# Cross-attention and LoRA-MoE on one core: three of eight delta additions of the last two pairs by way of ScalarE and GpSimd, and the sum of squares ahead of delta on TensorE

## The chip, the cores and the metric

The kernel runs on one core of one Trainium2 chip. The metric is the device time of the program in microseconds (us). The median of 3 runs of the kernel before is 455.8 us (454.64 to 456.86).

## What is computed

x and ctx are (8, 512, 2048) float32. Cut to what matters:

```python
x = x + xattn(layernorm(x), ctx, ctx)     # 8 heads of 64 channels: softmax over the head's channels for q,
                                          # over the 2048 positions for k; kv = k^T v, out = q kv
h = layernorm(x)
gates  = softmax of the top 2 of h @ router_w.T         # 4 experts
mid    = einsum('tf,erf->ter', h, A)                    # rank 16
x = x + 4 * einsum('te,ter,eor->to', gates, mid, B)     # "delta"
```

## The kernel before, in words

The 4096 rows (b, c) make 32 tiles of 128 (NT = 32), two tiles make a pair (NP = 16). A tile's 2048 columns are worked on in 16 chunks of 128, four chunks being a quarter. Every engine runs the same loop over steps q from -8 to 153, and each helper decides from q which tile and quarter (or pair) is its own, so the order on every engine is fixed by hand. Engines wait for each other by counting semaphores; each engine executes its own program in order.

For a tile: GpSimd subtracts the key maximum from ctx (`shift`, L311), ScalarE takes exponentials of keys and queries, TensorE makes kv and the numerator, VectorE normalises into `attnT` (L700), and GpSimd adds attnT to x, which gives x1 in `y_sb` (`add_x`, L323; four `attnT` slots, one for each quarter). ScalarE squares x1 (L544), TensorE folds the squares (`fold_squares`, L438), ScalarE copies the folded rows to `sq_sum` (`copy_squares`, L564), and TensorE sums them into a column of `raw_ps` (`sum_squares`, L448). `project` (L423) puts mid and the router's logits into the same `raw_ps`.

For a pair, p, the gates follow on single steps. At q = 8p+17: `gate_centre` (VectorE, L716 and L717, waits for the sum of squares of both tiles) makes the negative mean and E[x^2]; `root2` (GpSimd, L338 to L343) makes 1/sqrt(var); VectorE's `gate_logits` and `gate_below`. At 8p+18: VectorE's `gate_beats`, `gate_mask`, `gate_rank` (L758), ScalarE's `gate_exp` (L574, waits for root2), VectorE's `gate_select` (L763, waits for rank and exp), `gate_sum`, `gate_scale`. At 8p+19: `gate_mid` (L786), TensorE's `turn_mid` (L457). At 8p+20: `mid_high` (ScalarE, L583) and `mid_low` (VectorE, L800). From q = 8p+21 on `delta`: the pair's delta in eight groups i = 0 to 7, one a step. A group is four matmuls (L471 and L472) into one of two banks, `delta_ps[i % 2]`. VectorE adds it to `y_sb` (`add_delta`, L709) and frees the bank by counting `out_made`; TensorE's group i waits until group i-2 is added. Group i of pair p is written D(p,i) below. D(14,i) has q = 133+i and D(15,i) has q = 141+i. So the gates of pair 15 (q = 137 to 140) lie among the groups of pair 14.

Within a step TensorE issues delta, turn_max, sum_squares, numerator, spread_kmax, kv, project, fold_squares, turn_mid. The sums of squares of tiles 29, 30 and 31 have q = 128, 132 and 136. VectorE issues gate_beats(0), gate_mid, the maxima, kv_recip, gate_centre, gate_beats(1), gate_mask, mid_low, bn_part, add_delta, gate_logits, gate_rank, normalise, gate_below, gate_select, gate_sum, gate_scale. GpSimd issues root1, shift, root2, add_x.

SyncE issues all DMAs in order. For pair 14 two stores of 512 KB wait for the first four groups, and two (L243) for all eight; then pair 15 goes out in eight stores of 256 KB, one for each group (`store_last`, L248).

Of the kernel before, what the change touches and what calls it, by code (L numbers as in the profile page):

```python
# [6 lines left out]
ALU = mybir.AluOpType  # L7
# [32 lines left out]
def after(eng, sem, value):  # L40
    if value > 0:
        eng.wait_ge(sem, value)


def xattn_lora_moe_kernel(nc, x, xt, ctxt, wt, bt, consts, out):
# [7 lines left out]
    x_rows = x.rearrange("b c n -> (b c) n")  # L53
    FIRST = -8
    LAST = 4 * (NT - 1) + 29

    with ExitStack() as stack:
        def sb(name, shape, dt=F32):
# [5 lines left out]
        def sem(name):  # L64
            return stack.enter_context(nc.semaphore(name))
# [100 lines left out]
        rden_made = sem("rden_made")  # L166
        attn_made = sem("attn_made")
        out_made = sem("out_made")
        b_lo_made = sem("b_lo_made")
        negmean2_made = sem("negmean2_made")  # L170
        ex2_made = sem("ex2_made")
# [24 lines left out]
        def tile_at(q, offset):  # L196

            t, g = divmod(q - offset, 4)
            return (t, g) if 0 <= t < NT else (None, g)
# [6 lines left out]
        def delta_at(q):  # L206
            p, i = divmod(q - 21, 8)
            return (p, i) if 0 <= p < NP else (None, i)

        def chunks(g):  # L210
            return slice(g * CH, (g + 1) * CH)
# [4 lines left out]
        def pair_slots(p):  # L216
            return slice(2 * (p % 4), 2 * (p % 4) + 2)
# [3 lines left out]
        @block.sync  # L221
        def _(sp):
            PIECES = 2
            CP = NCH // 2 // PIECES
            XW = N // PIECES
            YC = NCH // PIECES

            def load_ctx(t, k):
                c = slice(k * CP, (k + 1) * CP)
                sp.dma_start(ctx_sb[:, t % 4, c, :, :].rearrange("p a c b -> p a (c b)"),  # L230
                             ctxt[t][:, c, :, :].rearrange("p a c b -> p a (c b)")).then_inc(ctx_landed[t % 4], 16)

            def load_x(t, k):
                c = slice(k * XW, (k + 1) * XW)
                sp.dma_start(x_sb[:, t % 4, c], x_rows[t * P:(t + 1) * P, c]).then_inc(x_landed[t % 4], 16)  # L235

            def load_y(t, k):
                c = slice(k * YC, (k + 1) * YC)
                sp.dma_start(y_sb[:, t % 8, c, :], xt[t][:, c, :]).then_inc(y_landed[t % 8], 16)

            def store(t, k):
                c = slice(k * YC, (k + 1) * YC)
                sp.dma_start(out[t, :, c, :].rearrange("p j c -> p (j c)"),  # L243
                             y_sb[:, t % 8, c, :].rearrange("p j c -> p (j c)")).then_inc(out_stored[t % 8], 16)

            def store_last(i):
                c = slice(2 * i, 2 * i + 2)
                sp.dma_start(out[NT - 2:NT, :, c, :].rearrange("t p j c -> p t (j c)"),  # L248
                             y_sb[:, pair_slots(NP - 1), c, :].rearrange("p t j c -> p t (j c)")
                             ).then_inc(last_stored, 16)  # L250

            def whole(load, t):
                for k in range(PIECES):
                    load(t, k)

            def quarters_done(q, offset):

                return min(q - offset + 1, 4 * NT)

            sp.dma_start(cst[:], consts).then_inc(cst_landed, 16)  # L260
            whole(load_ctx, 0)
            whole(load_x, 0)
            whole(load_ctx, 1)
            sp.dma_start(w_sb[:], wt).then_inc(w_landed, 16)
            whole(load_x, 1)
            whole(load_ctx, 2)
            whole(load_y, 0)
            sp.dma_start(b_rows, bt).then_inc(b_landed, 16)
            whole(load_y, 1)
            whole(load_x, 2)  # L270
            whole(load_ctx, 3)
            STEP = 4 // PIECES
            for q in range(0, 4 * NT + 28, STEP):
                last = q + STEP - 1
                p, r = divmod(q - 26, 8)
                if 0 <= p < NP - 1:
                    t, k = 2 * p + r // STEP % 2, r // (2 * STEP)
                    after(sp, raw_done, quarters_done(q - 1, 7))
                    sp.wait_ge(out_made, 8 * p + 8 // PIECES * (k + 1))
                    store(t, k)  # L280
                t, r = divmod(q + 10, 4)
                if 3 <= t < NT:
                    after(sp, num_done, 4 * (t - 4) + r + STEP)
                    load_x(t, r // STEP)
                t, r = divmod(q, 4)
                if 2 <= t < NT:
                    after(sp, raw_done, quarters_done(q, 7))
                    if t >= 8:
                        sp.wait_ge(out_stored[t % 8], 16 * PIECES * (t // 8))
                    load_y(t, r // STEP)  # L290
                t, r = divmod(q + 16, 4)
                if t < NT:
                    sp.wait_ge(kv_done, 4 * (t - 4) + r + STEP)
                    load_ctx(t, r // STEP)
            for i in range(8):
                sp.wait_ge(out_made, 8 * (NP - 1) + i + 1)
                store_last(i)
            for k in range(8):
                uses = len(range(k, NT - 2, 8))
                sp.wait_ge(out_stored[k], 16 * PIECES * uses)  # L300
            sp.wait_ge(last_stored, 16 * 8)

        @block.gpsimd
        def _(pool):
# [28 lines left out]
            def root2(q):  # L333
                p = pair_at(q, 13)
                if p is None:
# [7 lines left out]
                pool.tensor_tensor(rstd2[:], var2e[:], minus_half.to_broadcast([P, 2]),  # L343
                                   ALU.pow).then_inc(rstd2_made, 1)

            pool.memset(kv_sb[:], 0.0).then_inc(kv_zeroed, 1)
            pool.wait_ge(kv_zeroed, 1)
            for h in range(2):
# [4 lines left out]
            for q in range(FIRST, LAST + 1):  # L353
                root1(q)
                shift(*tile_at(q, -3))
                root2(q)
                add_x(*tile_at(q, 5))

        @block.tensor
        def _(pe):  # L360
# [98 lines left out]
            def delta(p, i):  # L459
                if p is None:  # L460
                    return
                if i == 0:
                    pe.wait_ge(lo_made, p + 1)
                    if p == 0:
                        pe.wait_ge(b_hi_made, 1)
                        pe.wait_ge(b_lo_made, 4)
                after(pe, out_made, 8 * p + i - 1)
                for k in range(2):
                    j = 2 * i + k
                    to = delta_ps[i % 2][:, k * 2 * P:(k + 1) * 2 * P]  # L470
                    pe.matmul(to, b_hi[:, j * P:(j + 1) * P], midT[:, p % 2, :], start=True, stop=False)  # L471
                    mm = pe.matmul(to, b_lo[:, j * P:(j + 1) * P], midT[:, p % 2, :], start=False, stop=True)  # L472
                mm.then_inc(delta_done, 1)
# [8 lines left out]
            for _ in range(40):  # L482
                pe.transpose(raw_ps[0][:, 0, 0:P], ident, ident)
            for q in range(FIRST, LAST + 1):
                delta(*delta_at(q))
                turn_max(q)
                sum_squares(q)
                if q == 1:
                    sum_w()
                numerator(*tile_at(q, 5))  # L490
                spread_kmax(q)
                kv(*tile_at(q, 0))
                project(*tile_at(q, 7))
                fold_squares(q)
                turn_mid(q)

        @block.scalar
        def _(act):
# [68 lines left out]
            def gate_exp(q):  # L567
# [5 lines left out]
                for d in range(2):  # L573
                    act.activation(gexp[:, d, :], below_max[:, d, :], ACT.Exp,  # L574
                                   scale=rstd2[:, d:d + 1]).then_inc(gexp_made, 1)

            def mid_high(q):
                p = pair_at(q, 16)
                if p is None:
                    return  # L580
                act.wait_ge(midT_done, 2 * p + 2)
                after(act, delta_done, 8 * (p - 1))
                act.activation(midT[:, p % 2, :].rearrange("p (d c) -> p d c", d=2),  # L583
                               raw_ps[p % 2][:, :, COL_MID:COL_MID + P], ACT.Copy).then_inc(hi_made, 1)
# [4 lines left out]
            for q in range(FIRST, LAST + 1):  # L589
# [14 lines left out]
                if r == 3:  # L604
                    copy_squares(T - 2)
                    keys(T + 1, 0)
                    queries(T, 0)
                if q == 2:
                    act.wait_ge(w_summed, 1)
                    act.activation(w_mean[:], raw_ps[1][:, 0, 0:ER + E], ACT.Copy,  # L610
                                   scale=1.0 / N).then_inc(w_mean_made, 1)
# [5 lines left out]
        def _(dve):  # L617
# [85 lines left out]

            def add_delta(p, i):
                if p is None:
                    return
                dve.wait_ge(delta_done, 8 * p + i + 1)
                y = y_sb[:, pair_slots(p), 2 * i:2 * i + 2, :]
                dve.tensor_tensor(y, delta_ps[i % 2][:].rearrange("p (j t c) -> p t j c", j=2, t=2), y,  # L709
                                  ALU.add).then_inc(out_made, 1)  # L710
# [186 lines left out]
```

## Time and profile before

| | us |
|---|---|
| median of 3 runs | 455.8 (454.64 to 456.86) |
| profiled execution | 454.94 |
| its span, first to last instruction | 453.2 |
| TensorE matmul busy | 422.5 (93%) |
| VectorE busy | 379.1 (84%) |
| GpSimd busy | 358.9 (79%) |
| ScalarE busy | 311.0 (69%) |

The profile is one execution; the median is over other executions of the same program. Busy times don't count waiting. In the rows PE is TensorE's matmuls, PEld its weight loads, DVE VectorE, ACT ScalarE, POOL GpSimd, SP SyncE, and SPq the queue of DMAs that SyncE issues. The granted clock is a share of TensorE's full 2.4 GHz.

### The profile page before, as it was taken

The numbers are of one execution on the slowest core, as the hardware profiler recorded it, in microseconds if no ns is written. First come the engines' busy times: TensorE is split into PE (matmuls) and PEld (weight loads), VectorE is DVE, ScalarE is ACT, GpSimd is POOL, SyncE is SP. The second block draws the span as 40 slices with busy tenths as digits, with TensorE's granted clock in tenths as the row PEclk, the third lists the DMA queues.
The fourth block names the chain that finished last, engine by engine and source line by source line (L and its number), as shares of the span: only waits on it lengthen the run. The fifth ranks groups of instructions, "written<-read, shape, count | busy, mean of one in ns | idle before, by whom it ended". The sixth has DMA issues, their size and how long they took to land.

```text
span 453.2 us, 16801 instructions
## 1 busy us (share of the span) xinstructions
PE 422.5 (93%) x6888; PEld 382.3 (84%) x6888; DVE 379.1 (84%) x1045; ACT 311.0 (69%) x436; POOL 358.9 (79%) x343
## 2 busy tenths in 40 slices
PE   6558998999999999999999999999999999999975
PEld 6557887898989898998989898998989898999864
DVE  3468777898998989898998989898989989775864
ACT  1265979695968778695958777785959777775310
POOL 0466999999898989898898989898988988994610
PEclk9667999999999999999999999999999999999988
DMA  8995888779999999999999999999999998454247
GB/s 286 420 409 188 307 290 271 248 276 321 364 297 372 339 340 344 307 341 332 351 310 361 331 346 341 307 352 333 357 316 338 310 366 269 173 186 187 95 185 279
DMA packets 38972, 137.59 MB, mean 304 GB/s; under 512 B 4208, under 2 KB 6384, under 8 KB 38768
## 3 DMA queue, kind: packets, MB, share of 16 engines
q1 hardware_dynamic: 38896, 136.52, 86.5%
q8 instruction: 55, 0.90, 0.8%
q14 instruction: 21, 0.17, 0.1%
HBM read 102.95 MB, written 33.55 MB: 301 GB/s over the span
## 4 chain that ended last, share of the span: by engine, by line
PE 71%; DVE 10%; POOL 6%; DMA 4%; issue 3%; SPq 3%; ACT 1%; POOLq 0%; DVEq 0%; ACTq 0%
PE num_ps L407 21%; PE kv_ps L390 14%; PE raw_ps L423 11%; PE delta_ps L471 10%; PE kv_ps L438 6%; PE delta_ps L472 6%; DMA ctx_sb<-in_ctxt_dram 4%; DVE y_sb L709 3%; POOL y_sb L323 3%; POOL ek_sb L311 3%; DVE attnT L700 2%; DVE bn_parts L642 2%; DVE midT L800 1%; PE raw_ps L457 1%; SPq L235 1%
## 5 line engine op out<-in xcount | busy, mean ns | idle before, releaser
L311 POOL TENSOR_TENSOR ek_sb<-ctx_sb,kmax_row 128x512 f32<-128x512 f32 x128 | 167.8, 1313 | 36.5 <-ACT kmax_row L504 36.5
L323 POOL TENSOR_TENSOR y_sb<-attnT,y_sb 128x512 f32<-128x512 f32 x128 | 164.3, 1284 | 31.0 <-DVE attnT L700 31.0
L407 PE MATMUL num_ps<-kv_sb,x_sb 128*128 128x130 f32 x1024 | 141.1, 281 | 9.0 <-DVE attnT L700 6.0
L407 PEld LDWEIGHTS num_ps<-kv_sb,x_sb 128*128 128x128 f32 x1024 | 126.0, 192 | 12.9 <-issue 8.7
L709 DVE TENSOR_TENSOR y_sb<-delta_ps,y_sb 128x512 f32<-128x512 f32 x128 | 87.3, 684 | 23.7 <-PE delta_ps L472 22.8
L625 DVE TENSOR_REDUCE max_n<-ctx_sb 128x32 f32<-128x512 f32 x128 | 86.5, 677 | 10.8 <-DMA ctx_sb<-in_ctxt_dram 10.8
L390 PE MATMUL kv_ps<-ctx_sb,ek_sb 128*64 128x65 f32 x2048 | 92.8, 233 | 0.3 <-ACT ek_sb L526 0.3
L700 DVE TENSOR_TENSOR attnT<-num_ps,rden 128x512 f32<-128x512 f32 x128 | 88.5, 691 | 4.8 <-DVE rden L697 0.4
L390 PEld LDWEIGHTS kv_ps<-ctx_sb,ek_sb 128*64 128x64 f32 x2048 | 74.2, 139 | 17.8 <-issue 5.8
L526 ACT ACTIVATE ek_sb<-ek_sb 128x1024 f32<-128x1024 f32 x64 | 67.1, 1049 | 26.9 <-POOL ek_sb L311 26.9
L423 PE MATMUL raw_ps<-w_sb,y_sb 128*64 128x69 f32 x2048 | 84.5, 223 | 0.0
L471 PE MATMUL delta_ps<-midT,b_hi 128*128 128x256 f32 x256 | 81.1, 338 | 0.6 <-DVE y_sb L709 0.4
L533 ACT ACTIVATE x_sb<-x_sb,nbias,rstd 128x1024 f32<-128x1024 f32 x64 | 78.8, 1231 | 0.0
L423 PEld LDWEIGHTS raw_ps<-w_sb,y_sb 128*64 128x64 f32 x2048 | 73.1, 136 | 0.9
L472 PE MATMUL delta_ps<-midT,b_lo 128*128 128x256 f32 x256 | 68.0, 287 | 0.0
L471 PEld LDWEIGHTS delta_ps<-midT,b_hi 128*128 128x128 f32 x256 | 49.5, 193 | 13.2 <-issue 5.8
L472 PEld LDWEIGHTS delta_ps<-midT,b_lo 128*128 128x128 f32 x256 | 50.0, 195 | 0.0
L642 DVE BATCH_NORM_STATS2 bn_parts<-x_sb 128x6 f32<-128x512 f32 x64 | 43.9, 686 | 1.0 <-DMA x_sb<-in_x_dram 0.5
L544 ACT ACTIVATE sq_b<-y_sb 128x1024 f32<-128x1024 f32 x32 | 33.7, 1052 | 6.1 <-POOL y_sb L323 6.1
L564 ACT ACTIVATE sq_sum<-kv_ps 128x128 f32<-128x128 f32 x32 | 8.5, 266 | 38.3 <-PE kv_ps L438 38.3
L697 DVE RECIPROCAL rden<-num_ps 128x8 f32<-128x8 f32 x128 | 25.7, 201 | 10.6 <-PE num_ps L407 9.8
L544 ACT ACTIVATE sq_a<-y_sb 128x1024 f32<-128x1024 f32 x32 | 33.5, 1048 | 0.0
(63 smaller groups left out, 398.3 us busy)
## 6 DMA issues: line engine op xcount, KB each, us to landing
ctx_sb<-in_ctxt_dram SPq DMA_DIRECT2D x64, 520.0 KB, 5.3
x_sb<-in_x_dram SPq DMA_DIRECT2D x64, 512.0 KB, 6.1
y_sb<-in_xt_dram SPq DMA_DIRECT2D x64, 512.0 KB, 6.3
out_dram<-y_sb SPq DMA_DIRECT2D x60, 512.0 KB, 6.2
out_dram<-y_sb SPq DMA_DIRECT2D x8, 256.0 KB, 3.6
sq_a<-in_bt_dram SPq DMA_DIRECT2D x1, 1024.0 KB, 15.8
w_sb<-in_wt_dram SPq DMA_DIRECT2D x1, 552.0 KB, 9.6
cst<-in_consts_dram SPq DMA_DIRECT2D x1, 145.0 KB, 2.3
```

Source lines behind the costliest of these rows:

```text
L311: pool.tensor_tensor(ek_sb[:, t % 2, chunks(g), :].rearrange("p (a b) c -> p a b c", b=2), ctx_sb[:, t % 4, 2 * g:2 * g + 2, 1:P + 1, :].r ...
L323: pool.tensor_tensor(y, attnT[:, g, :], y, ALU.add).then_inc(x1_made, 1)
L390: mm = pe.matmul(kv_ps[t % 2][d, h:h + DH + 1], ek_sb[:, t % 2, j, d], ctx_sb[:, t % 4, j // 2, v, j % 2], start=(j == 0), stop=(j == NCH ...
L407: mm = pe.matmul(num_ps[:, j // 2, at:at + 2 * (DH + 1)], x_sb[:, t % 4, c * P:(c + 1) * P], kv_sb[:, t % 2, :], start=True, stop=True, sk ...
L423: mm = pe.matmul(raw_ps[p % 2][c, odd, 0:NQ], y_sb[:, t % 8, j, c], w_sb[:, j, :], start=(odd == 0 and j == 0), stop=(j == NCH - 1), skip_ ...
L471: pe.matmul(to, b_hi[:, j * P:(j + 1) * P], midT[:, p % 2, :], start=True, stop=False)
L472: mm = pe.matmul(to, b_lo[:, j * P:(j + 1) * P], midT[:, p % 2, :], start=False, stop=True)
L533: act.activation(half, half, ACT.Exp, bias=nbias1[:, t % 4:t % 4 + 1], scale=rstd1[:, t % 4:t % 4 + 1]).then_inc(q_made, 1)
L544: act.activation(to, y_sb[:, t % 8, 8 * h:8 * h + 8, :].rearrange("p j c -> p (j c)"), ACT.Square).then_inc(sq_made, 1)
L625: dve.tensor_reduce(max_n[:, t % 2, c], ctx_sb[:, t % 4, :, 1 + g * 32:33 + g * 32, :].rearrange("p a c b -> p c a b"), AX.XY, ALU.max).th ...
L700: dve.tensor_tensor(attnT[:, g, :].rearrange("p (b k d) -> p b k d", b=2, d=DH), heads[:, :, :, 0:DH], rden[:].unsqueeze(3).to_broadcast([ ...
L709: dve.tensor_tensor(y, delta_ps[i % 2][:].rearrange("p (j t c) -> p t j c", j=2, t=2), y, ALU.add).then_inc(out_made, 1)
```

## The change

In pairs NP-2 = 14 and NP-1 = 15, three groups each (1, 3, 5 and 0, 2, 4) are no longer added by VectorE. ScalarE copies the bank into one of the four `attnT` slots (`copy_delta`, after all of x1 has been made), which frees the bank (`delta_copied`), and GpSimd adds the slot to `y_sb` (`add_delta_late`, last in its step). `adds_until` says how many adds up to a group are VectorE's and how many the other way's; SyncE's stores and TensorE's delta wait for both counts. From q = 4 NT = 128 on, TensorE issues sum_squares ahead of delta.

```diff
@@ kernel
+    BY_POOL = {NP - 2: (1, 3, 5), NP - 1: (0, 2, 4)}
...
+        def by_pool(p, i):
+            return i in BY_POOL.get(p, ())
+
+        def adds_until(p, i):
+
+            n = 8 * p + i + 1
+            shared = sum(1 for pair in BY_POOL for k in BY_POOL[pair] if 8 * pair + k < n)
+            return n - shared, shared
@@ SyncE, store of pairs 0 to 14
-                    sp.wait_ge(out_made, 8 * p + 8 // PIECES * (k + 1))
+                    by_dve, shared = adds_until(p, 8 // PIECES * (k + 1) - 1)
+                    sp.wait_ge(out_made, by_dve)
+                    after(sp, out_made_pool, shared)
@@ SyncE, the last eight stores
-                sp.wait_ge(out_made, 8 * (NP - 1) + i + 1)
+                by_dve, shared = adds_until(NP - 1, i)
+                sp.wait_ge(out_made, by_dve)
+                after(sp, out_made_pool, shared)
                 store_last(i)
@@ GpSimd
+            def add_delta_late(p, i):
+
+                if p is None or not by_pool(p, i):
+                    return
+                n = adds_until(p, i)[1]
+                pool.wait_ge(delta_copied, n)
+                y = y_sb[:, pair_slots(p), 2 * i:2 * i + 2, :]
+                pool.tensor_tensor(y, attnT[:, (n - 1) % 4, :].rearrange("p (j t c) -> p t j c", j=2, t=2), y,
+                                   ALU.add).then_inc(out_made_pool, 1)
...
                 root2(q)
                 add_x(*tile_at(q, 5))
+                add_delta_late(*delta_at(q))
@@ TensorE, delta
-                after(pe, out_made, 8 * p + i - 1)
+                by_dve, shared = adds_until(p, i - 2)
+                after(pe, out_made, by_dve)
+                after(pe, delta_copied, shared)
@@ TensorE, the loop
             for q in range(FIRST, LAST + 1):
+                if q >= 4 * NT:
+                    sum_squares(q)
                 delta(*delta_at(q))
                 turn_max(q)
-                sum_squares(q)
+                if q < 4 * NT:
+                    sum_squares(q)
@@ ScalarE
+            def copy_delta(p, i):
+
+                if p is None or not by_pool(p, i):
+                    return
+                n = adds_until(p, i)[1]
+                act.wait_ge(x1_made, 4 * NT)
+                after(act, out_made_pool, n - 4)
+                act.wait_ge(delta_done, 8 * p + i + 1)
+                act.activation(attnT[:, (n - 1) % 4, :], delta_ps[i % 2][:], ACT.Copy).then_inc(delta_copied, 1)
...
                     keys(T + 1, 0)
                     queries(T, 0)
+                copy_delta(*delta_at(q))
@@ VectorE, add_delta
                 if p is None:
                     return
+                if by_pool(p, i):
+                    return
```

## Rows read from the trace of the kernel before

**Rows 1.** Busy time by stretch (us, instructions; then granted clock, DMA share, GB/s).
```profile
300.00:400.00 100.00, 98.31 (x1678) 89.38 (x1670) 90.10 (x254) 75.53 (x107) 88.22 (x85) 1.00 0.90 309
...
434.00:440.00 6.00, 3.28 (x22) 2.73 (x21) 5.44 (x21) 0.49 (x3) 1.10 (x3) 0.88 0.45 178
440.00:446.00 6.00, 5.92 (x26) 5.07 (x26) 3.98 (x7) 0.38 (x1) 0.00 (x0) 0.55 0.60 226
```

**Rows 2.** Chain of waits, 437 to 442: start, us, what ran.
```profile
437.47 0.23 DVE raw_ps L758
...
437.72 0.18 DVE gsel L763
...
438.73 0.50 DVE mid L786 x2
...
439.27 0.70 PE raw_ps L457 x2
...
440.41 0.44 DVE midT L800
...
440.90 0.58 PE delta_ps L471
441.48 0.21 PE delta_ps L472
```

**Rows 3.** Busy time by stretch, 442 to 452.
```profile
442.00:443.00 1.00, 1.00 (x6) 0.78 (x5) 0.69 (x1) 0.00 (x0) 0.00 (x0) 0.50 0.56 225
443.00:444.00 1.00, 1.00 (x5) 1.00 (x6) 0.69 (x1) 0.00 (x0) 0.00 (x0) 0.50 1.00 401
...
450.00:451.00 1.00, 0.00 (x0) 0.00 (x0) 0.00 (x0) 0.00 (x0) 0.00 (x0) 1.00 1.02 350
451.00:452.00 1.00, 0.00 (x0) 0.00 (x0) 0.00 (x0) 0.00 (x0) 0.00 (x0) 1.00 0.37 128
```

**Rows 4.** Instructions in order of time, 433 to 437: start, us, engine, line.
```profile
433.28 0.28 ACT L564 ACTIVATE sq_sum<-kv_ps 128x128 f32<-128x128 f32 x1 [1.20 <-PE kv_ps L438]
...
433.93 1.29 DVE L709 TENSOR_TENSOR y_sb<-delta_ps,y_sb 128x512 f32<-128x512 f32 x2 [1.92 <-PE delta_ps L472]
...
434.09 0.28 PE L472 MATMUL delta_ps<-midT,b_lo 128*128 128x256 f32 x1
...
434.20 0.28 PE L448 MATMUL raw_ps<-cst,sq_sum 128*128 128x2 f32 x2
...
435.13 0.15 DVE L716 TENSOR_SCALAR negmean<-raw_ps 128x2 f32<-128x2 f32 x1
...
435.36 0.19 POOL L338 TENSOR_TENSOR mean_sq<-negmean 128x2 f32<-128x2 f32 x1 [4.37 <-DVE negmean L716]
...
435.97 0.71 POOL L343 TENSOR_TENSOR rstd<-var2e,cst 128x2 f32<-128x2 f32 x1
...
436.71 0.49 ACT L574 ACTIVATE gexp<-below_max,rstd 128x4 f32<-128x4 f32 x2 [3.15 <-POOL rstd L343]
```

**Rows 5.** Groups by line and shape, 395 to 453: count | busy, mean ns.
```profile
L323 POOL TENSOR_TENSOR y_sb<-attnT,y_sb 128x512 f32<-128x512 f32 x13 | 16.6, 1278 | 10.6 <-DVE attnT L700 10.6
...
L533 ACT ACTIVATE x_sb<-x_sb,nbias,rstd 128x1024 f32<-128x1024 f32 x5 | 6.1, 1229 | 0.0
...
L544 ACT ACTIVATE sq_b<-y_sb 128x1024 f32<-128x1024 f32 x4 | 4.2, 1055 | 6.1 <-POOL y_sb L323 6.1
...
L583 ACT ACTIVATE midT<-raw_ps 128x256 fp32r<-128x256 f32 x3 | 1.2, 385 | 5.3 <-PE raw_ps L457 5.3
```

**Rows 6.** Last stores and adds: order of time, then the store line's own view.
```profile
441.64 0.81 SPq L243 DMA_DIRECT2D out_dram<-y_sb  x2
...
447.42 1.33 DVE L709 TENSOR_TENSOR y_sb<-delta_ps,y_sb 128x512 f32<-128x512 f32 x2 [0.19 <-PE delta_ps L472]
...
L248 SPq DMA_DIRECT2D out_dram<-y_sb x8: 401/496/1062, 442.9 to 448.8; - x8
...
DMA to landing us min/median/max: 3.1/3.6/4.0
```

More of the change, by code:

```diff
@@ L168, in xattn_lora_moe_kernel @@
         out_made = sem("out_made")
+        out_made_pool = sem("out_made_pool")
+        delta_copied = sem("delta_copied")
         b_lo_made = sem("b_lo_made")
```

## The prediction

> D(p,i) is delta group i of pair p, and the step numbers q are those of the section on the kernel. Times are us from the start of the span.
>
> **What bounds the kernel now.** I read the busy time by stretch first. In the body (300 to 400) TensorE is busy 98.3 of 100 us at full clock; none of the diff's branches fires there, since GpSimd takes groups of pairs 14 and 15 alone and the order on TensorE changes only from q = 128 on. At the end the picture is another: TensorE is busy 3.28 of 6.00 between 434 and 440, where VectorE is busy 5.44, and 5.92 of 6.00 between 440 and 446, at a granted clock of 0.55 (nearly all of it at 1.2 GHz of 2.4) [rows 1]. So only the last 20 us are at stake, and in their middle a serial chain counts. The chain of waits shows it: softmax gates of pair 15 on VectorE (gsel at 437.72, mid at 438.73), the transpose of mid on TensorE at 439.27, the high part on ScalarE, the low part on VectorE at 440.41, and D(15,0) on TensorE at 440.90 [rows 2]. Third, the DMA by stretch: share 0.56 in 442:443, 1.00 in 443:444, 1.02 in 450:451, 0.37 in 451:452 [rows 3]. The last 3.1 MB (two stores of 512 KB, eight of 256 KB) leave in one unbroken stream. It starts when D(14,7) is added, as the two large stores wait for it and D(14,7) stands behind the transpose of mid on TensorE. Hence the end follows the moment at which the gate chain of pair 15 is through, nearly whatever the adds of pair 15 do.
>
> **Parts that move nothing.** The extra waits of SyncE and TensorE split one semaphore's count over two; for pairs 0 to 13 the second has the value zero and isn't waited for. Sum_squares at q = 128 and 132 goes ahead of D(13,3) and D(13,7): the same two short matmuls, 0.28 in the record [rows 4], in either place. VectorE reads the first a step later, behind a normalise that waits for TensorE anyway, and the second only with tile 31's. Zero for both; were that cover gone, under 0.28 each.
>
> **The squares of tile 31 (q = 136).** Before, D(14,3) runs first (its last matmul 434.09 to 434.37) and the sum of squares starts at 434.20 and is done at 434.48 [rows 4]. Its input sq_sum is made at 433.28 + 0.28 = 433.56, before D(14,3)'s first matmul, three steps of 0.12 (as from 434.09 to 434.20) ahead of its last: 433.73. So in the new order it starts at 433.73 and is done at 434.01, and D(14,3) is done two such steps later, at 434.60. By itself this earlier sum is worth nothing: gate_centre starts at 435.13, well behind it, because VectorE is in two adds from 433.93 on for 1.29 [rows 4]. With D(14,3)'s add gone from VectorE, gate_centre can start after one of them, at about 434.55, 0.58 earlier.
>
> **The price of a copy and of a GpSimd add.** An ACT copy of 128x512 from PSUM isn't in the trace. Nearest below: 128x128 from PSUM, 0.28 [rows 4]; above: 128x1024 in SBUF, 1.055, and with bias and scale 1.229 [rows 5]. On the line between the copy of 128x256 from PSUM (0.385) and the 1024 wide one, 512 is 0.385 + 256 x (1.055 - 0.385)/768 = 0.61. I take 0.60; the ends are 0.28 and 1.23. The GpSimd add has the size and both SBUF inputs of L323: 1.28 [rows 5], and its ends are that and the 1.30 to which I round it up for the other pattern of columns. VectorE did two in 1.29.
> The Trainium skill, page "ScalarE: Activation LUTs", section "Rules for kernel authors", budgets about 0.3 us for an ACTIVATE plus 0.83 ns an element, an estimate of 0.73 for the copy; for the 1024 wide ones it gives 1.15, where the trace has 1.055 and 1.229. By that rule the shift below would be 0.77 where the rows give 0.64.
>
> **The stall that the change adds.** The copy of D(14,1) on ScalarE falls into the 1.20 for which that engine is idle ahead of copy_squares at 433.28 [rows 4]; it runs 432.1 to 432.7, so that isn't late. GpSimd's add is 432.75 to 434.03. The second is the one that bites: D(14,3) is done at 434.60, copied by 435.22, added on GpSimd 435.25 to 436.53. In GpSimd's program this add (q = 136) stands ahead of root2 of pair 15 (q = 137). Root2 began at 435.36 with mean_sq, its power ended at 435.97 + 0.71 = 436.68, and exp began at 436.71 [rows 4]. Now root2 starts at 436.50, 1.14 later, although its input is ready 0.58 earlier. So the power ends at 437.82, exp runs 437.85 to 438.34, and gate_select, at 437.72 before, waits for it and starts at 438.36: **0.64 late**. VectorE can't win that back: the three adds taken off it lie ahead of this wait (rank, at 437.47 before [rows 2], would start at about 437.0). Behind gate_select all steps shift by the 0.64: mid at 439.37, transpose at 439.91, D(15,0) at 441.54 [rows 2]. D(14,5)'s copy stands behind exp on ScalarE and is done at about 438.95, its GpSimd add at 440.25: TensorE needs the bank for D(14,7) only after the transpose, and SyncE wants the add at 442.2. Both covered by over a microsecond. The stores of the first half of pair 14 go out once D(14,3) is added, at 436.6, five microseconds ahead of the next ones, into a half idle stretch of the DMA engines: nothing.
>
> **The drain of pair 15.** D(14,7) is added by 442.2 where it was by 441.6, so the two large stores leave from 442.28 on (were from 441.64 on [rows 6]), and the stream begins at 443.1 instead of 442.45 (a share of 0.56 in 442:443 [rows 3]). TensorE at the low clock spends 4 x 0.215 = 0.86 on a group [rows 2]. With two engines emptying the two banks, each bank is free about when TensorE comes back: group starts at 441.54, 442.40, 443.26, 444.23, 445.09, 446.04, then, at the full clock, 446.74 and 447.46. VectorE's last add ends at 448.82; before it was 447.42 + 1.33 = 448.75 [rows 6]. VectorE's share of the drain thus wins the 0.64 back but for 0.07. But the store of an even group waits for copy and GpSimd: D(15,4) is copied by 446.7 and added by 448.0, so its store is issued at 448.05; SyncE issues in order, and the four last stores, 0.50 each [rows 6], come at 448.05, 448.55, 449.05 and 449.55. The last was at 448.8. The stream needs its 8.9 us (442.45 to 451.37 before [rows 3]) from 443.1 on and ends at 452.0, and no store comes so late that the engines run dry by more than 0.1. A store's landing, 3.1 to 4.0 [rows 6], holds that queueing already. Either reading gives 0.6 to 0.75 later.
>
> **Sum.** Body 0; squares 0; root2 behind the second GpSimd add +0.64; drain 0 on the stream of stores: span 453.2 + 0.64 = 453.8. The profiled execution took 454.94 (1.74 around the span), so 455.6 for it. It lies 0.86 under the median of the timed runs, so for the median I forecast 455.8 + 0.64 = 456.4. With a copy at 0.28 the shift is 0.32, with 1.23 it is 1.27 and the drain no longer hides.
>
> **Rivals.**
> *The intended gain arrives.* If root2 isn't held, gate_select comes with rank, whose start falls from 437.47 [rows 2] to about 437.0 since D(14,5)'s add is gone: 0.5 earlier, span 452.7, median 455.3. For it: VectorE is the busy engine between 434 and 440 [rows 1]. Against: to have exp done by 437.2 GpSimd must start its add by 434.1, and D(14,3) isn't in PSUM then. Chance 0.12.
> *The stream of stores decides alone, nothing moves.* If stores that come spread out leave at the 401 GB/s of 443:444 rather than at the 350 of 450:451 [rows 3], a stream of 3.1 MB is shorter by up to 1.1 and makes up for the later start; half of that leaves the end within 0.1 of before: 455.8. For it: those two rates. Against: all the bytes must still leave after a later start. Chance 0.15.
> *The copy holds the banks; slower beyond what can be told.* Place: the copy of even groups of pair 15, in front of TensorE's next even group. At 1.23 a copy, TensorE waits 0.6 more before D(15,2), D(15,4) and D(15,6), of which 1.2 stays, and root2 comes another 0.63 late: 0.64 + 0.63 + 1.2 = 2.5, span 455.7, median 458.3. It decides from a copy of about 0.85, where TensorE's 0.86 no longer covers it. Against: the line through the two PSUM copies, 0.28 and 0.385 for 128 and 256 columns, gives 0.60 for 512. Chance 0.07.
> *The clock stays low.* Granted clock is 0.55 in 440:446 [rows 1] after the idle ahead of the transpose; that idle grows by 0.64. If the full clock doesn't come back before the end, the last three groups take 0.86 each: last add 449.4 to 449.9, span 454.4 to 454.9, median about 457.2. For it: the gap grows. Against: TensorE then works as densely as before. Chance 0.11.
> The Trainium skill, page "TensorE: Matmul & The Clock Gate", section "What's actually happening", says that the gated clock is the default and that activity lifts it, which fits the fall after the idle in this trace and would favour this last case.
>
> **Chances and range.** Forecast 0.55, the four rivals 0.12, 0.15, 0.07 and 0.11. All but one lie within 0.5% (2.3 us), about what a measurement of this kernel can tell from no change; the timed runs of one kernel lay 2.2 apart. Faster by over 0.5%: 0.04, for the spread of a median alone. Slower by over 0.5%: 0.07. Within: 0.89. Range 454.6 to 458.0: from the gain with 0.7 of spread below it to the low clock with 0.8 above.
>
> **What would show it.** Right: on GpSimd, the add of D(14,3) followed without a gap by mean_sq at about 436.5; ScalarE's exp and VectorE's gsel at 437.85 and 438.4, with gsel released by exp; D(15,0) at about 441.5; copies of 0.6; stores ending at 449.5 or later. Wrong: mean_sq before 435.4, gsel under 437.7, D(15,0) before 440.9 or after 442.2, copies above 0.85, or a difference ahead of 425.

## The result and the profile after

The changed kernel is slower: median 458.10 us of 22 runs against 456.59 us for the kernel before, ratio 1.0045 (95% interval 1.0029 to 1.0062), that is 2.0 us (1.3 to 2.8). A second series gave 1.0032 (1.0017 to 1.0047), 1.5 us. Together, each series weighted by its interval, about 1.7 us. The forecast was +0.64 on a median of 455.8 from three runs; 22 runs put that median at 456.59. The three-run median was 0.8 low.

The profiled execution of the changed kernel took 457.65 us. The page's head:

```profile
span 455.9 us, 16833 instructions
...
PE 422.8 (93%) x6888; PEld 382.4 (84%) x6888; DVE 375.1 (82%) x1039; ACT 314.6 (69%) x442; POOL 366.9 (80%) x349
```

The span is 2.7 longer, but that isn't the change. Up to the last normalise of tile 31 (VectorE, attnT) both kernels execute the same instructions in the same order, except for where two sums of squares (q = 128 and 132, two short matmuls each) stand. It came at 428.94 before and here at:

```profile
430.32 0.69 DVE L743 TENSOR_TENSOR attnT<-num_ps,rden 128x512 f32<-128x512 f32 x1
```

1.38 later. The prediction named a difference ahead of 425 as a sign of being wrong, so this needs a reason. Over the 17 profiles of this document it lies between 428.94 and 432.25: 428.94 to 430.91 in the five kernels that leave the squares in their old place, 429.00 to 432.25 in the twelve others, so it doesn't follow the change. It goes with the time that TensorE spent at the low clock ahead of it: 20.5 us in five profiles, with the last normalise at 428.9 to 430.2, and 30.7 us in six, with it at 430.3 to 432.3 (correlation 0.8 over the 17). Part of it is visible in the granted clock at the start, here after and then before, stretch 20:40 (us; busy by engine; granted clock, DMA share, GB/s):

```profile
20.00:40.00 20.00, 15.25 (x125) 13.77 (x124) 12.96 (x24) 10.50 (x13) 9.20 (x7) 0.50 0.85 334
```

```profile
20.00:40.00 20.00, 14.40 (x130) 12.99 (x131) 13.06 (x25) 10.50 (x13) 9.21 (x7) 0.60 0.84 331
```

So every time below is counted **from the start of the last normalise** ("from N"). The tail from N to the end is 24.2 before and 25.6 after, 1.3 more (24.21 and 25.55). In order of time (start, us, engine, line), the part that answers to [rows 4]:

```profile
434.66 0.28 ACT L596 ACTIVATE sq_sum<-kv_ps 128x128 f32<-128x128 f32 x1 [0.71 <-PE kv_ps L465]
...
435.10 0.28 PE L475 MATMUL raw_ps<-cst,sq_sum 128*128 128x2 f32 x2
...
435.30 0.69 DVE L754 TENSOR_TENSOR y_sb<-delta_ps,y_sb 128x512 f32<-128x512 f32 x1 [3.22 <-PE delta_ps L501]
...
435.91 0.15 DVE L761 TENSOR_SCALAR negmean<-raw_ps 128x2 f32<-128x2 f32 x1
...
436.06 0.60 ACT L617 ACTIVATE attnT<-delta_ps 128x512 f32<-128x512 f32 x1 [1.12 <-PE delta_ps L501]
...
436.74 1.28 POOL L369 TENSOR_TENSOR y_sb<-attnT,y_sb 128x512 f32<-128x512 f32 x1 [1.43 <-ACT attnT L617]
...
437.97 0.20 POOL L354 TENSOR_TENSOR mean_sq<-negmean 128x2 f32<-128x2 f32 x1
...
438.36 0.23 DVE L803 TENSOR_REDUCE raw_ps<-beats_m 128x8 f32<-128x64 f32 x1
438.59 0.71 POOL L359 TENSOR_TENSOR rstd<-var2e,cst 128x2 f32<-128x2 f32 x1
439.33 0.48 ACT L606 ACTIVATE gexp<-below_max,rstd 128x4 f32<-128x4 f32 x2 [2.67 <-POOL rstd L359]
...
439.92 0.17 DVE L808 SCALAR_TENSOR_TENSOR gsel<-raw_ps,gexp 128x8 f32<-128x8 f32 x1 [1.33 <-ACT gexp L606]
...
441.46 0.44 PE L484 MATMUL raw_ps<-cst,mid 128*128 128x128 f32 x2 [3.16 <-DVE mid L831]
...
442.84 0.58 PE L500 MATMUL delta_ps<-midT,b_hi 128*128 128x256 f32 x1 [0.46 <-DVE midT L845]
```

The sum of squares (L475) is ahead of D(14,3), and gate_centre starts 5.59 from N (6.19 before). Its result waits: GpSimd is in the add of D(14,3) and starts mean_sq with the add's end, at 7.65 (6.42 before). Rank is ready at 8.04, but gate_select starts at 9.60 and follows exp, where before it was 8.78 and followed rank: 0.82 late. D(15,0) starts at 12.52 (11.96), only 0.56 late. The other 0.26 came back between them, since the transpose of mid (L484) took 0.44 at the full clock where it took 0.70 at the low one before [rows 2].

The last stores: SyncE's queue in order of time, the store line's own view (ns min/median/max of an issue) and the DMA in two stretches, against [rows 6] and [rows 3]:

```profile
446.18 6.31 SPq L260 DMA_DIRECT2D out_dram<-y_sb  x8
```

```profile
L260 SPq DMA_DIRECT2D out_dram<-y_sb x8: 372/422/1157, 446.2 to 452.0; - x8
...
DMA to landing us min/median/max: 2.3/3.1/3.5
```

```profile
448.00:449.00 1.00, 0.61 (x6) 0.51 (x5) 0.69 (x1) 0.38 (x1) 0.71 (x2) 1.00 0.70 231
...
451.00:452.00 1.00, 0.00 (x0) 0.00 (x0) 0.00 (x0) 0.00 (x0) 0.00 (x0) 1.00 0.57 190
```

VectorE's last add ends at 20.24 from N (19.81 before), the last store is issued at 452.0, 21.7 from N (19.9 before). The DMA engines ran dry twice, share 0.70 and 0.57, where the stream had been unbroken. Over the whole stream, from the first packet of the two large stores to the last packet of all, before and then after:

```profile
442.46:452.33 9.87, 5.41 (x27) 4.35 (x26) 5.12 (x8) 0.00 (x0) 0.00 (x0) 0.85 0.92 320
```

```profile
444.40:455.05 10.65, 4.55 (x27) 3.74 (x26) 3.36 (x5) 1.55 (x3) 3.85 (x3) 0.82 0.85 297
```

The bytes are the same and take 9.0 us of the DMA engines in both. The stream starts 0.56 later from N (14.08 against 13.52) and is 0.8 longer, all of it idle time. These two make up the 1.3 by which this profile ends later. In the second profile of the changed kernel they are 0.6 and 0.3.

### The profile page after: what moved, and what is told of

Read it like the earlier page. It is cut to its first block, busy times and chain, and to the rows that moved or that the text cites. A ratio compares the mean times of both kernels' runs of the same rounds, so it can differ in the third digit from the quotient of the medians.

```text
span 455.9 us, 16833 instructions
## 1 busy us (share of the span) xinstructions
PE 422.8 (93%) x6888; PEld 382.4 (84%) x6888; DVE 375.1 (82%) x1039; ACT 314.6 (69%) x442; POOL 366.9 (80%) x349
## 4 chain that ended last, share of the span: by engine, by line
PE 71%; DVE 9%; POOL 7%; DMA 4%; issue 3%; SPq 3%; ACT 2%; DVEq 0%; ACTq 0%; POOLq 0%
PE num_ps L434 22%; PE kv_ps L417 13%; PE raw_ps L450 11%; PE delta_ps L500 9%; PE kv_ps L465 6%; PE delta_ps L501 6%; DMA ctx_sb<-in_ctxt_dram 4%; POOL y_sb L339 3%; POOL ek_sb L327 3%; DVE attnT L743 2%; DVE y_sb L754 2%; DVE bn_parts L685 2%; SPq L247 1%; PE raw_ps L484 1%; DVE midT L845 1%
## 5 line engine op out<-in xcount | busy, mean ns | idle before, releaser
L754 DVE TENSOR_TENSOR y_sb<-delta_ps,y_sb 128x512 f32<-128x512 f32 x122 | 83.3, 683 | 27.3 <-PE delta_ps L501 26.4
L500 PE MATMUL delta_ps<-midT,b_hi 128*128 128x256 f32 x256 | 80.1, 335 | 1.4 <-ACT attnT L617 0.8
L740 DVE RECIPROCAL rden<-num_ps 128x8 f32<-128x8 f32 x128 | 25.6, 200 | 12.5 <-PE num_ps L434 11.7
```

## The experiments

All times in the table are one profile each, counted from N; "last add" is the end of VectorE's last, "store" the start of the last store's issue, "ratio" that of timed runs to the kernel before in the same series. One profile's times behind gate_select can't be read to better than half a microsecond: kernel 1 has gate_select where the kernel before has it, but its granted clock stayed full until 11.9 from N (9.6 in the kernel before), and its D(15,0) and its last add come 0.3 and 0.5 earlier.

| kernel | gate_select | D(15,0) | last add | store | end | ratio (95%) |
|---|---|---|---|---|---|---|
| before | 8.78 | 11.96 | 19.81 | 19.9 | 24.2 | 1 |
| changed | 9.60 | 12.52 | 20.24 | 21.7 | 25.6 | 1.0045 (1.0029 to 1.0062) |
| changed, again | 9.60 | 12.55 | 19.92 | 21.4 | 25.1 | 1.0032 (1.0017 to 1.0047) |
| 1 squares only | 8.76 | 11.69 | 19.34 | 19.8 | 24.1 | 1.0007 (0.9988 to 1.0026) |
| 2 pair 14 only | 9.58 | 12.51 | 20.12 | 20.3 | 25.3 | 1.0036 (1.0014 to 1.0057) |
| 3 pair 15 only | 8.76 | 11.68 | 19.40 | 19.9 | 23.3 | 0.9995 (0.9978 to 1.0012) |
| 4 root2 first | 8.29 | 11.22 | 18.94 | 20.0 | 23.6 | 1.0004 (0.9985 to 1.0023) |
| 5 root2 first, pair 14 | 8.30 | 11.22 | 18.86 | 18.9 | 23.7 | 0.9998 (0.9978 to 1.0017) |
| 6 store order | 9.58 | 12.75 | 20.48 | 20.6 | 25.3 | 1.0025 (1.0009 to 1.0040) |
| 7 before, D(14,7) early | 8.77 | 11.97 | 20.31 | 20.3 | 23.4 | 0.9989 (0.9971 to 1.0008) |
| 8 root2 first, D(14,7) early | 8.30 | 11.51 | 19.00 | 20.9 | 24.5 | 1.0009 (0.9988 to 1.0030) |
| 9 before, hold of two adds | 10.76 | 13.93 | 21.30 | 22.1 | 26.4 | 1.0043 (1.0028 to 1.0058) |
| 10 before, hold of one add | 9.53 | 12.45 | 20.78 | 20.8 | 24.8 | 1.0018 (1.0003 to 1.0032) |
| 11 before, gaps filled | 8.77 | 11.69 | 18.44 | 19.3 | 23.0 | 0.9979 (0.9963 to 0.9996) |
| 12 changed, gaps filled | 9.60 | 12.53 | 19.28 | 21.0 | 25.0 | 1.0018 (1.0001 to 1.0035) |
| 13 root2 first, gaps filled | 8.30 | 11.23 | 17.99 | 18.8 | 22.7 | 0.9963 (0.9945 to 0.9980) |
| 14 root2 first, pair 14, D(14,7) early, filled | 8.28 | 11.49 | 18.12 | 18.1 | 23.1 | 0.9983 (0.9962 to 1.0004) |

Part of the spread of the timed runs goes with TensorE's mean granted clock in a run: over the 314 runs of the four later series (all but the first of the changed kernel, in which the clocks of the kernel before weren't recorded) a run is 1.3 us shorter for each 0.01 more of it. An estimate with this taken out (one slope for all, one base for each series) is given below as "at equal clock"; its intervals are 0.5 either way.

**1. Squares only.**
```diff
-    BY_POOL = {NP - 2: (1, 3, 5), NP - 1: (0, 2, 4)}
+    BY_POOL = {}
```


> Only the order of the sums of squares is changed; VectorE makes all adds. Theory A (the whole loss sits behind step 133, in two places: root2 of pair 15 queued behind GpSimd's second add, and the last stores queued in SyncE behind GpSimd's adds of pair 15): within 0.3 us of the kernel before, mean_sq at the same distance behind the adds of pair 14 as before. Rival B (a loss of the program as such, spread over the body or the start, which one profile pair showed as 1.4 us ahead of step 133): 1 us or more slower than before even here.


+0.3 us (-0.5 to +1.2), at equal clock +0.2, mean_sq at 6.51 (6.42 before). The order of the squares is worth nothing and costs nothing measurable, and rival B's 1 us or more doesn't show.

**2 and 3. One pair each.**
```diff
+    BY_POOL = {NP - 2: (1, 3, 5)}     # 2
+    BY_POOL = {NP - 1: (0, 2, 4)}     # 3
```


> Pair 14 by way of ScalarE and GpSimd, pair 15 all on VectorE. Theory A: +0.6 to +0.8 us against before: root2 waits for the add of D(14,3), D(15,0) starts 0.6 later than before against the adds of pair 14, the drain (first matmul of D(15,0) to the last store's issue) stays at 7.9 as before. Rival C (only the drain costs): 0 +-0.3. Rival B: as large as the whole change, about +2.

> Pair 15's groups 0, 2, 4 by way of ScalarE and GpSimd, pair 14 all on VectorE. Theory A: the gate chain is as before; from D(15,0) to the last store's issue 9.0 to 9.3 us instead of 7.9, of which the landing of the last store gives back 0.6: +0.6 to +1.2 us against before. Rival D (only the held root2 costs; the drain is hidden under the stream of stores as I forecast): 0 +-0.3.


Pair 14 alone +1.6 (+0.6 to +2.6), pair 15 alone -0.2 (-1.0 to +0.5). Gate_select is late with pair 14 (9.58) and in time with pair 15 (8.76). Pair 14 costs more than the 0.6 to 0.8 expected, though the interval reaches down to it. The second half of theory A, that pair 15's drain costs 0.6 to 1.2 by itself, missed. That the profile of kernel 3 ends 0.9 earlier than before is no gain to count on: its execution took 2.3 us more than its span, where the others took 1.7 to 1.9 more.

**4 and 5. Root2 ahead of the late adds.**
```diff
-                add_delta_late(*delta_at(q))
+                add_delta_late(*delta_at(q - 1))     # 4; 5 with pair 14 alone
```


> The changed kernel with GpSimd's late adds issued one step later, so that root2 of pair 15 stands ahead of the add of D(14,3). Theory A: gate_select comes with rank, 1.0 to 1.3 us earlier against the adds of pair 14 than in the changed kernel; the chain is 0.5 ahead of the kernel before; the drain still costs: between -0.2 and +0.8 us against before, 1.1 less than the changed kernel. Rival C (only the drain costs): no difference to the changed kernel's +2.

> Pair 14 by way of ScalarE and GpSimd, pair 15 on VectorE, and the late adds one step later, behind root2. Theory A2 (the whole loss is root2 of pair 15 held behind the add of D(14,3)): gate_select about 0.47 earlier after the last normalise than in the kernel before (8.3 against 8.8), total -0.5 us against before, 2 less than with pair 14 alone and root2 behind. Rival E (it is the extra load of ScalarE and GpSimd in pair 14, whatever the order): stays near +1.5.


GpSimd, ScalarE and VectorE of kernel 4 in order of time:

```profile
432.25 0.69 DVE L743 TENSOR_TENSOR attnT<-num_ps,rden 128x512 f32<-128x512 f32 x1
...
438.06 0.20 POOL L354 TENSOR_TENSOR mean_sq<-negmean 128x2 f32<-128x2 f32 x1 [0.84 <-DVE negmean L761]
...
439.35 1.28 POOL L369 TENSOR_TENSOR y_sb<-attnT,y_sb 128x512 f32<-128x512 f32 x1
...
440.28 0.23 DVE L803 TENSOR_REDUCE raw_ps<-beats_m 128x8 f32<-128x64 f32 x1
440.54 0.17 DVE L808 SCALAR_TENSOR_TENSOR gsel<-raw_ps,gexp 128x8 f32<-128x8 f32 x1
```

mean_sq now starts right behind gate_centre, the add of D(14,3) comes after root2, and gate_select follows rank at 8.29. The same work in another order takes the loss away: +0.2 (-0.7 to +1.1) and -0.1 (-1.0 to +0.8), that is 1.3 to 1.8 under the same kernel with root2 behind the add (the changed kernel and kernel 2). The slow store issue is in both profiles too (1.01 us in kernel 4, 1.46 in kernel 5). Rivals C and E fall. The 0.5 that the chain is ahead of the kernel before doesn't show in the times; the intervals would just hide it.

**9 and 10. The hold alone, in the kernel before.**
```diff
+                if q == 8 * (NP - 1) + 17:
+                    pool.wait_ge(out_made, 8 * (NP - 2) + 4)
+                    for n in range(2):                   # 10: range(1)
+                        pool.tensor_tensor(attnT[:, n, :], attnT[:, 2, :], attnT[:, 3, :], ALU.add).then_inc(held, 1)
                 root2(q)
```


> The kernel before, all adds on VectorE, with two spare GpSimd adds of 128x512 in front of root2 of pair 15, released when D(14,3) is added. Their results are used by nothing. Theory A2: root2 starts 2.5 us after D(14,3)'s add, that is 2.5 later than before, exp and gate_select come 2.0 later, and the total is 2.0 us (1.7 to 2.6) over before. Rival E: gate_select late but the total within 0.5 of before, since ScalarE and VectorE carry nothing more.

> The kernel before with one spare GpSimd add of 128x512 in front of root2 of pair 15, released by the add of D(14,3): root2 starts 7.6 after the last normalise, as in the changed kernel, gate_select at 9.6. If the hold passes through one to one and no more: +0.8 us. If a hold of this size costs more than itself, as the changed kernel's 1.5 to 2.0 suggests: +1.3 or more. If the excess of the changed kernel comes from its drain: +0.8 here.


Kernel 10, in order of time:

```profile
430.91 0.69 DVE L706 TENSOR_TENSOR attnT<-num_ps,rden 128x512 f32<-128x512 f32 x1
...
437.26 1.28 POOL L360 TENSOR_TENSOR attnT<-attnT 128x512 f32<-128x512 f32 x1 [4.30 <-DVE y_sb L715]
...
438.50 0.19 POOL L339 TENSOR_TENSOR mean_sq<-negmean 128x2 f32<-128x2 f32 x1
...
440.44 0.17 DVE L769 SCALAR_TENSOR_TENSOR gsel<-raw_ps,gexp 128x8 f32<-128x8 f32 x1 [0.79 <-ACT gexp L580]
```

Gate_select is 1.98 late with two spare adds and 0.75 with one; the total is +2.0 (+1.3 to +2.6) and +0.8 (+0.1 to +1.5). So a late root2 by itself costs time, and within these intervals it passes through one to one. Of the changed kernel's 1.7 the hold alone gives 0.8. Whether the other 0.9 lies elsewhere isn't settled: the intervals of kernel 10 and of the changed kernel overlap, and at equal clock they are +0.9 and, for the second series, +1.3.

**6. Stores in the order of the adds.**
```diff
-            for i in range(8):
+            for i in (1, 0, 3, 2, 5, 4, 6, 7):
                 by_dve, shared = adds_until(NP - 1, i)
-                sp.wait_ge(out_made, by_dve)
-                after(sp, out_made_pool, shared)
+                if by_pool(NP - 1, i):
+                    sp.wait_ge(out_made_pool, shared)
+                else:
+                    sp.wait_ge(out_made, by_dve)
```


> The changed kernel with SyncE issuing the last eight stores in the order in which their groups were added (1, 0, 3, 2, 5, 4, 6, 7), each waiting for its own engine alone. Theory Q (the late stores queue in SyncE behind group 4's, which GpSimd ends 1.3 us after VectorE would, and the DMA engines run dry): the last store's issue comes 0.5 to 1.0 earlier and the total is 0.4 to 0.9 under the changed kernel. Rival (the end follows the gate chain alone): equal to the changed kernel.


The last store is issued 0.7 to 1.1 earlier (20.6 from N), yet its issue took 1.36 us and it landed 4.2 later, so the profile's end stayed at 25.3. +1.1 (+0.4 to +1.8) against +1.5 for the changed kernel in the same series, with medians of 457.80 and 457.76: not separated. Theory Q, with its 0.4 to 0.9, isn't borne out, nor is it ruled out.

**7 and 8. D(14,7) ahead of the transpose of mid.**
```diff
@@ TensorE
-                delta(*delta_at(q))
+                if q != LATE_Q:                      # 8 * (NP - 1) + 20
+                    delta(*delta_at(q))
...
+                if q == LATE_Q - 1:
+                    delta(*delta_at(LATE_Q))
                 turn_mid(q)
```
VectorE's add of D(14,7) is moved ahead of mid_low in the same way; kernel 8 is kernel 4 with this.


> The kernel before with one thing changed: TensorE issues D(14,7) ahead of the transpose of pair 15's mid, and VectorE adds it ahead of mid_low. Nothing of the gate chain moves. Theory S (the end follows the unbroken stream of stores, which starts when D(14,7) is added, as in my prediction): the two large stores leave 1.5 to 2.5 us earlier and the end comes 1.0 to 2.0 us earlier. Rival T (the end follows the last add and its store): within 0.3 of before.

> The changed kernel with root2 ahead of the late adds and D(14,7) ahead of the transpose of mid on TensorE and ahead of mid_low on VectorE. Theory S: 1.5 to 2.5 us under the kernel before. Rival T: what root2 first alone gave (+0.2), less at most 0.3.


-0.5 (-1.3 to +0.4; at equal clock -0.6) and +0.4 (-0.5 to +1.4). The large stores leave earlier, and then the DMA engines wait for the adds. Kernel 7 in two stretches (granted clock, DMA share, GB/s last):

```profile
442.50:443.50 1.00, 1.00 (x5) 0.77 (x5) 0.84 (x2) 0.00 (x0) 0.00 (x0) 0.50 0.98 401
...
445.50:446.50 1.00, 1.00 (x6) 1.00 (x6) 0.54 (x2) 0.00 (x0) 0.00 (x0) 0.50 0.64 217
```

Kernel 8 is the clear miss of theory S, on which my treatment of the drain rested: -1.5 to -2.5 expected, +0.4 measured. So the start of the stream alone doesn't set the end. Kernel 7 is less clear: its stream starts 1.2 earlier from N than in the kernel before, loses 0.4 of that to idle DMA engines, and its profile ends 0.8 earlier, although its last add is 0.5 later (the low clock lasted until 18.2 from N, before until 16.5). Its time separates neither theory S (-1.0 to -2.0) nor rival T (within 0.3) from what was measured.

**11, 12, 13 and 14. Spare transposes in TensorE's idle time.**
```diff
+            def fill(n):
+                pe.wait_ge(attn_made, 4 * NT)
+                for _ in range(n):
+                    pe.transpose(num_ps[:, 0, 0:P], ident, ident)
...
+                if q == 8 * (NP - 1) + 19:
+                    fill(14)                         # 12: 22, 13: 12
                 turn_mid(q)
+                if q == 8 * (NP - 1) + 20:
+                    fill(3)
```


> The kernel before with 14 spare transposes ahead of the transpose of mid and 3 behind D(14,7), in TensorE's idle time; results unused. If the low clock in the drain costs: the first groups of pair 15 take 0.5 rather than 0.86 on TensorE, the drain is bound by VectorE at 0.76 a group, last add 1.0 to 1.8 after D(15,0) earlier; total -1.0 to -1.6 if the last add sets the end, -0.2 to -0.5 if the stream of stores does.

> The changed kernel with 22 spare transposes ahead of the transpose of mid and 3 behind D(14,7), results unused. If the excess over the 0.8 of the gate chain is the low clock in the drain: it goes, and the total is 0.8 above the filled kernel before, that is about -0.1 against before. If it is the copies and GpSimd adds of the drain: it stays, +0.4 or more against before.

> Root2 ahead of the late adds, both pairs by way of GpSimd, and 12 plus 3 spare transposes in TensorE's gaps. If gate chain (-0.5) and clock (-0.95, as in the filled kernel before) add up: -1.4 us against before. If the drain by GpSimd costs 0.5: -0.9.

> Pair 14 by way of GpSimd with root2 first, D(14,7) ahead of the transpose, and spare transposes in the three gaps (6, 3, 8): everything that should pull the end in. Gate chain -0.5, large stores 2 us earlier, drain at full clock: 2.0 to 3.0 us under before if each part counts; if TensorE is late by the spare work it shows as D(15,0) later than 11.2 after the last normalise.


Kernel 11, TensorE in order of time, then its clock in the stretch of the drain:

```profile
438.65 1.69 PE L484 MATMUL num_ps<-cst 128*128 128x128 f32 x14
...
442.51 0.39 PE L471 MATMUL delta_ps<-midT,b_hi 128*128 128x256 f32 x1
```

```profile
442.00:446.00 4.00, 3.76 (x23) 2.73 (x22) 3.66 (x6) 0.00 (x0) 0.00 (x0) 1.00 0.51 200
```

The granted clock stays at 1.00 (2.4 GHz) in 442:446, where it was 0.55 in the same work before [rows 1]. The drain from D(15,0) to the last add takes 6.75 instead of 7.85, and the total is -1.0 (-1.7 to -0.2). Kernel 12 is +0.8 (0.0 to +1.6) and thus 1.8 over kernel 11, of another series, where 0.8 was expected if the low clock were the changed kernel's excess. That speaks against the clock. Kernel 13 is -1.7 (-2.5 to -0.9), faster than both kernels. Kernel 14 has 6 transposes ahead of D(14,7), 3 behind it and 8 behind that of mid; it gave -0.8 (-1.7 to +0.2), less than its parts.

Kernels 12 and 13 run the same instructions from D(15,0) on, and at the same distances: last add at 6.75 and 6.76 behind D(15,0). Yet their medians, of one series, are 2.6 apart (457.18 and 454.55), where D(15,0) is 1.3 apart. They differ in the place of root2 and in the number of spare transposes ahead of mid's (22 and 12). From the spread of 12 runs each the 2.6 is known to 0.7, so here a loss beyond the chain's 1.3 is clear of noise. Their store line, 12 first:

```profile
L260 SPq DMA_DIRECT2D out_dram<-y_sb x8: 372/447/1369, 446.5 to 452.1; - x8
```

```profile
L260 SPq DMA_DIRECT2D out_dram<-y_sb x8: 372/452/660, 444.2 to 449.0; - x8
```

In 12 one of eight issues takes 1369 ns, in 13 the longest is 660. The last store is issued 1.74 behind the last add in 12, 0.85 in 13, and the end is 12.4 against 11.5 behind D(15,0). The whole stream of stores takes 10.0 us in 12, 9.3 in 13 and 8.9 in 11. In kernel 3, whose profile ends early too, the longest issue is 468 ns.

**The changed kernel again.**


> The changed kernel once more, for a second estimate of the whole. Theory A3 (the hold of the gate chain passes through one to one, 0.8 us, and the drain by way of GpSimd adds about 0.5 on top): ratio to before 1.002 to 1.004. If the loss is the hold alone: 1.0018. If something spread over the body is at work: 1.0045 again with the last normalise later than in the other kernels.


+1.5 (+0.8 to +2.1). The last normalise at 430.7 is inside the spread of the others; so nothing points to a loss spread over the body.

## Why the prediction was right or wrong

- **The body and the squares.** Right: kernel 1 is +0.3 with zero inside its interval, and gate_centre came at 5.59 from N, where the forecast's 434.55 is 5.61.
- **Price of a copy and of an add.** Right: copies 0.57 to 0.60, GpSimd adds 1.26 to 1.29. The 0.73 that I drew from the Trainium skill's rule (page "ScalarE: Activation LUTs", section "Rules for kernel authors") is too high here; the trace decides for 0.60. The rule's 0.3 us holds for an ACTIVATE whose bias is a pointer operand, a condition that I left out and that this copy doesn't meet.
- **Root2 held behind the add of D(14,3).** The mechanism is right and shown from both sides: taken away by order alone (4, 5), put into the kernel before alone (9, 10). The size was off: I forecast mean_sq, exp and gate_select at 7.56, 8.91 and 9.42 from N, and they came at 7.65, 9.01 and 9.60. Half of the difference is the 0.59 from exp's start to gate_select's, for which I had 0.51; before, gate_select waited for rank and exp's own delay was hidden. The term is 0.82, not 0.64. By luck D(15,0) came nearly as forecast all the same (12.52, and 12.60 forecast), because the transpose of mid ran at the full clock in this profile.
- **The drain.** This is the step that failed: "drain 0 on the stream of stores", with "no store comes so late that the engines run dry by more than 0.1". In the profile of the changed kernel the DMA engines were idle for 0.8 us more within the stream than before, and for 0.3 in its second profile. The sum counted only the later start of the stream; the end depends on the last adds and their stores too, and kernel 8 shows that an earlier stream by itself brings nothing. In the kernel before, the last store goes out 0.05 behind the last add: SyncE waits for nearly each add, and a slow issue in the middle is hidden by that. Where GpSimd makes groups 0, 2 and 4, four stores come back to back at the end, and one slow issue among them moves the last: it starts 1.49 behind the last add in the changed kernel (I had 0.73), 1.44 in its second profile, 1.74 in kernel 12. The banks, too, weren't free "about when TensorE comes back": it waited 0.38 and 0.39 for the copies of D(15,2) and D(15,4).
- **What stays open.** The timed loss of 1.7 is 0.9 above what the hold gave alone. That the slow issue, or the drain by way of GpSimd, is this 0.9 isn't shown: no kernel took the slow issue away by itself, kernel 3 has the same drain with the gate chain in time and is at -0.2, kernel 4 has the drain and a slow issue and is at +0.2, and kernel 2 has the hold with VectorE's drain and is at +1.6. What the kernels with a loss share is an add ahead of root2, and with root2 first the loss is gone. That the loss hangs on that order is shown; why it is more than the 0.8 of gate_select isn't. In the unfilled kernels the extra may in part be noise; between kernels 12 and 13 it is clear of it: 1.3 beyond the chain's 1.3, of which their two profiles show 0.9, with a slow issue, behind D(15,0).
- **The rivals.** Once root2 is first, gate_select is 0.5 early, as the first rival had it, but no gain shows in the times of kernels 4 and 5. "The clock stays low" isn't what happened: the full clock came back 3.2 behind D(15,0) (4.5 before). Its price is real all the same: 1.0 us in the kernel before, as 11 shows. "The copy holds the banks" needed copies of about 0.85; with 0.60 they held TensorE for the 0.8 named above, not for 1.2 and a later root2.
- **The forecast of the time.** 458.1 lies 1.7 above the forecast. Of this 0.8 is the median of three runs on which it stood; the medians of 22 runs then differ by 1.5 where I had 0.64. Of these 0.9, 0.2 is the mis-sized hold, and the rest is what stays open above.

## What to carry to other kernels

Before work is moved to a less busy engine, look at the instruction that follows it in that engine's program: a 1.3 us add in front of three tiny ones on the critical chain cost 0.8 us by itself, and issuing it one step later left no loss that could be measured. Ask also what else is released late: stores that wait in order for a helper's later result came back to back at the end here. And compare two profiles from the last common event, not from the start: here identical code before it differed by up to 3.3 us.

## What the runs showed of the hardware

- Of the eight last stores of 256 KB, issued by SyncE, one (in kernel 9 two) took 1.0 to 1.6 us to issue, where most took 0.37 to 0.75, in 14 of 17 profiles; in kernel 10 the longest was 0.83, in 13 0.66 and in 3 0.47. It was the second in one kernel and the eighth in four, at no fixed time. Its cause is open.
- TensorE's granted clock stayed at 2.4 GHz through the drain when 17 transposes of 0.12 us filled its gaps (kernel 11; the same with 25, 15 and 17 of them in kernels 12 to 14), and the kernel gained 1.0 us (0.2 to 1.7) by work that nobody uses.
- Nominally equal executions differ by 3.3 us in when the last normalise starts (428.94 to 432.25), and the time at the low clock ahead of it, 20.5 to 30.7 us, goes with it (0.18 us later for each us of it, correlation 0.8). What else adds to it is open.
